# An adaLN block with a mixture of experts: a reordered last shared group, later down weights, tables in the experts' program, last tiles with kept numbers and in halves

## The reference

```python
h = _layernorm(x) * (1 + cb) + sb
scores = sigmoid(h @ gate_w + bias)
top_scores, top_idx = top_k(scores, 2)            # of 8 experts
top_scores = top_scores / (sum(top_scores) + 1e-06)
hact = gelu(h @ up_w[e] + up_b[e])                # per chosen expert, 256 -> 1024
eo = hact @ down_w[e] + down_b[e]                 # 1024 -> 256
shared = (gelu(h @ sw_up + sb_up) @ sw_down + sb_down) * 0.1
out = shared + sum(top_scores * eo * 0.1)
out = out / (max(abs(out)) + 1e-06)               # over the 256 numbers of a token
x = x + gb * out
```

## Time and profile before

| | us |
|---|---|
| median of 3 runs | 877.2 (875.07 to 881.87) |
| the profiled execution | 877.31 |
| its span | 875.4 |
| TensorE busy in the span | 828.9 (95%) |
| VectorE, ScalarE, POOL busy | 611.5, 455.1, 458.6 |
| mean granted TensorE clock | 0.978 of full speed |

### The profile page before, as it was taken

The page is one execution under the profiler, slowest core; times in us unless marked ns, Lnnn a source line. Parts: engine busy times, 40 slices in busy tenths (PEclk is TensorE's granted clock), DMA queues, the critical chain, the costliest instruction groups (busy, mean ns, idle before and its releaser), DMA issues.

```text
span 875.4 us, 21221 instructions
## 1 busy us (share of the span) xinstructions
PE 828.9 (95%) x5973; PEld 776.9 (89%) x5974; DVE 611.5 (70%) x1566; ACT 455.1 (52%) x859; POOL 458.6 (52%) x521
## 2 busy tenths in 40 slices
PE   6999999899999999999799999989999999999982
PEld 5778887889889989987799999979999999999982
DVE  5788988668777777767847566666666666666653
ACT  3865654244443544445476555565566555556630
POOL 4554320224765765675204656646656665665565
PEclk9999999899999999999999999989999999999996
DMA  8220000381242243232652333434433343444442
GB/s 300 75 97 1 1 0 1 89 253 25 101 125 38 88 123 77 67 103 91 227 198 76 89 88 98 147 96 94 94 86 86 87 93 93 92 92 86 86 89 52
DMA packets 68491, 83.25 MB, mean 95 GB/s; under 512 B 22976, under 2 KB 56730, under 8 KB 68288
## 3 DMA queue, kind: packets, MB, share of 16 engines
q0 software_dynamic: 25792, 39.92, 19.6%
q1 hardware_dynamic: 41808, 41.64, 15.1%
q10 hardware_dynamic: 816, 0.79, 0.3%
HBM read 45.43 MB, written 41.55 MB: 99 GB/s over the span
## 4 chain that ended last, share of the span: by engine, by line
PE 28%; issue 7%; DVE 4%; DMA 3%; ACT 3%; POOL 2%; DVEq 2%; ACTq 1%; POOLq 0%
PE psUp L1971 14%; PE psY L1996 13%; DMA gx<-shared_part,meta 2%; ACT gu L2034 1%; DVEq L995 1%; DMA shared_part<-ys,widx 1%; POOL out L2243 1%; PE psH L1943 1%; DVE gTl L2099 1%; ACT gTh L2039 1%; DVE yc L2120 1%; DVE top L2138 1%; POOL shared_part L2233 1%; DVE fin L2147 0%; ACTq L995 0%
## 5 line engine op out<-in xcount | busy, mean ns | idle before, releaser
L1971 PE MATMUL psUp<-eT,wup 128*128 128x256 f32 x1632 | 206.3, 287 | 5.5 <-DVE eT L2094 4.2
L1971 PEld LDWEIGHTS psUp<-eT,wup 128*128 128x128 f32 x1632 | 202.2, 195 | 6.5 <-issue 6.3
L1996 PE MATMUL psY<-wdn,gTh 128*128 128x256 f32 x1088 | 200.5, 286 | 0.0
L1996 PEld LDWEIGHTS psY<-wdn,gTh 128*128 128x128 f32 x1088 | 169.4, 192 | 0.0
L1996 PE MATMUL psY<-wdn,gTl 128*128 128x256 f32 x544 | 154.3, 284 | 0.0
L2243 POOL DMA_INDIRECT out<-fin,oidx x68 | 109.3, 1608 | 23.2 <-issue 15.9
L2034 ACT ACTIVATE gu<-psUp,ubias 128x256 f32<-128x256 f32 x272 | 113.4, 468 | 8.0 <-DVE gTl L2099 4.1
L2053 ACT ACTIVATE ys<-yc,meta 128x256 f32<-128x256 f32 x68 | 31.0, 503 | 162.6 <-DVE yc L2120 162.6
L2233 POOL DMA_INDIRECT shared_part<-ys,widx x68 | 71.4, 1050 | 79.5 <-issue 49.6
L2099 DVE TENSOR_TENSOR gTl<-gu,gTh 128x512 fp32r<-128x512 f32 x136 | 93.7, 689 | 27.4 <-ACT gTh L2039 24.7
L2224 POOL DMA_INDIRECT gx<-shared_part,meta x68 | 68.0, 1001 | 84.0 <-DMA shared_part<-ys,widx 62.3
(11 more groups left out here) (325 smaller groups left out, 1392.2 us busy)
## 6 DMA issues: line engine op xcount, KB each, us to landing
hin<-expert_in SPq DMA_DIRECT2D x36, 256.0 KB
X<-in_L_attn_x SPq DMA_DIRECT2D x8, 512.0 KB, 7.8
X<-bo_row POOLq DMA_DIRECT2D x8, 512.0 KB, 5.6
shared_part<-prow SPq DMA_DIRECT2D x8, 512.0 KB, 6.0
shared_part<-sh SPq DMA_DIRECT2D x8, 512.0 KB
out<-X SPq DMA_DIRECT2D x8, 512.0 KB, 4.3
raw_up<-in_L_ffn_up_w SPq DMA_DIRECT2D x3, 1024.0 KB, 5.6
raw_dn<-in_L_ffn_down_w SPq DMA_DIRECT2D x3, 1024.0 KB, 9.7
```

Of the source, the lines that this page charges most:

```text
L1971: mm = nc.tensor.matmul(psU[:, c, (m % 2) * TR:(m % 2 + 1) * TR], wup[s][:, a, k, m * P:(m + 1) * P], eT[:, u, b, k], start=(n == 0), stop ...
L1996: mm = nc.tensor.matmul(psE[:, u, h * C:(h + 1) * C], (gTh, gTl)[a][:, u, m, h * P:(h + 1) * P], wdn[s][:, b, m], start=(n == 0), stop=(n ...
```

## The change

It has these parts.

1. In the last shared group TensorE takes `up(3)` ahead of `rank()`. ScalarE takes the sigmoid after `gelu(1)`, not after `gelu(0)`, and the splits of the first expert's `raw_up` after `gelu(6)` and `gelu(7)`. VectorE's order changes as the diff shows, and `pos_ok` is given by `choose_rest`.
2. SP asks for `raw_dn` of the first expert behind the two loads of rows. In the experts' program it loads the rows of tile 2 and the last 16 numbers of each row of tile 1 (`meta`) first, then the second expert's weights, then the biases; the biases are waited for by tile 0's result.
3. `table_used`, `table_slots` and `table_next` run in the experts' program, after `low(0, 0)`. The engines wait for `tab_ok` 4 there, and tile 0 takes slot 0 without reading a table. `iota_h` is made in the shared program.
4. From tile 32 on, `known` keeps an entry in a register, so that it is read once on an engine; TensorE and VectorE read some of them ahead.
5. The last tile's end works by halves of 128 rows (`finish`): `g_in` is a semaphore per half, and POOL issues the first half's `out` when `fin` of that half is ready. POOL writes a tile's `ys` only if another tile follows, and ScalarE leaves the last tile's out.

```diff
-    def weights(sp, e):
+    def weights_up(sp, e):
         sp.dma_start(raw_up[:], up_v[bass.ds(e, 1)].rearrange("a p k n -> p (a k) n")).then_inc(up_in, 16)
+
+    def weights_dn(sp, e):
         sp.dma_start(raw_dn[:], down_v[bass.ds(e, 1)].rearrange("a p k n -> p (a k) n")).then_inc(dn_in, 16)
...
                 else:
                     up(2)
+                    up(3)
                     rank()
-                    up(3)
                     down(0)
                     down(1)
                 if ffn_on:
...
                     for m in range(MK):
                         gelu(m)
-                        if m == 0:
+                        if m == 1:
                             act.wait_ge(mx_ok, f + 1)
                             nc.scalar.activation(sg[:], mx[:, :, 0:TOPK].rearrange("p t k -> p k t"), ACT.Sigmoid
                                                  ).then_inc(sg_ok, 1)
-                        if m in (5, 6):
-                            split_hi(act, 0, 0, (0,), (m - 5,))
+                        if m >= MK - 2:
+                            split_hi(act, 0, 0, (0,), (m - MK + 2,))
                     return
...
-                    nc.vector.tensor_tensor(h2[:, r, :, C + 1:C + 1 + E], wd[:, 0], wd[:, 1], ALU.add)
+                    step(nc.vector.tensor_tensor(h2[:, r, :, C + 1:C + 1 + E], wd[:, 0], wd[:, 1], ALU.add))
+                    settled()
+                    assert n[0] == ROUTE + 5
+                    nc.vector.sem_inc(pos_ok, 1)
...
                 if not att_on:
                     gate_copy()
+                    shared_read(f - 1)
                     gate_read()
                     tops()
                     places()
                     choose_two()
-                    choose_rest()
-                    place()
-                    shared_read(f - 1)
                     low_g(0)
                     low_g(1)
+                    place()
+                    choose_rest()
                     low_g(2)
-                    dve.wait_ge(rt_dve, ROUTE * NG + 4)
                     table_experts()
                     low_g(3)
                     table_spans()
                     low_g(4)
                     table_rows()
                     low_g(5)
-                    table_used()
+                    low_g(6)
                     split_lo(dve, 0, 0, (0,), (0,))
-                    low_g(6)
-                    table_slots()
                     low_g(7)
-                    table_next()
                     split_lo(dve, 0, 0, (0,), (1,))
                     return
                 second = isinstance(g, int) and g == 1
...
-            weights(sp, entry(sp, etab, 0, E - 1))
+            e_first = entry(sp, etab, 0, E - 1)
+            weights_up(sp, e_first)
...
             for j in range(2):
                 load_rows(sp, first_rows[j], j)
+            weights_dn(sp, e_first)
...
+    def known(eng, table, j, most):
+
+        if not isinstance(j, int) or j < FULL:
+            return entry(eng, table, j, most)
+        key = (eng.engine, table.name, j)
+        for old in [k for k in held if k[0] == eng.engine and k[2] < j - 2]:
+            del held[old]
+        if key not in held:
+            held[key] = entry(eng, table, j, most)
+        return held[key]
...
             load_tails(sp, entry(sp, rtab, 0, E * REG - TR), 0)
             sp.wait_ge(sh_ev, 2 * NG)
             sp.dma_start(shd_v[:, TG * (NG - 1):NT, :], sh[:]).then_inc(sh_st, 16)
+            rows(2, 0)
+            tails(1, 1)
+            sp.wait_ge(tab_ok, 3)
+            e = entry(sp, ntab, 0, E - 1)
+            with sp.If_ne(sp.to_reg(e), 0):
+                sp.wait_ge(w_ok, 1)
+                weights_up(sp, e)
+                sp.wait_ge(w_ok, 2)
+                weights_dn(sp, e)
+            sp.wait_ge(tab_ok, 4)
             sp.dma_start(dbias[:], down_b.partition_broadcast(P)).then_inc(db_in, 16)
-            ahead(0)
             tiles(sp, body)
...
-                k_exp = entry(pe, ktab, j, E)
+                if isinstance(j, int) and j == 0:
+                    return 0, 0
+                k_exp = known(pe, ktab, j, E)
                 if isinstance(j, int) and j >= FULL:
-                    return entry(pe, stab, j, 2), k_exp
+                    return known(pe, stab, j, 2), k_exp
...
+            pe.wait_ge(tab_ok, 4)
 
             def body(j, u, more, i):
+                soon = isinstance(j, int) and FULL - 2 <= j < ET - 2
+                if soon:
+                    known(pe, stab, j + 2, 2)
                 if more:
                     up(j + 1, 1 - u)
+                if soon:
+                    known(pe, ktab, j + 2, E)
                 down(j, u, more, i)
 
             tiles(pe, body)
...
                 wait(dve, ey_mm, j + 1)
+                if isinstance(j, int) and j == 0:
+                    dve.wait_ge(db_in, 16)
                 if later(j, 1):
...
+            def finish(j, u, landed, h, e):
+
+                done = 3 * j + 3 * h
+                wait(dve, g_in[u][h], landed)
+                if not h:
+                    wait(dve, s_ok, 2 * j)
+                    wait(dve, f_s, 2 * j)
+                nc.vector.tensor_tensor(bs[:, h], gx[:, u, h, C:2 * C], gx[:, u, h, 0:C], ALU.add).then_inc(b_ok, 1)
+                wait(dve, ey_ev, j + 1)
+                wait(dve, b_ok, j + 1 + h)
+                nc.vector.scalar_tensor_tensor(sm[:, h], yc[:, h], meta[:, u, h, bass.ds(e + 1, 1)], bs[:, h],
+                                               ALU.mult, ALU.add).then_inc(s_ok, 1)
+                wait(dve, s_ok, 2 * j + h + 1)
+                nc.vector.tensor_reduce(top[:, 0, h:h + 1], sm[:, h], AX.X, ALU.max, apply_absolute_value=True
+                                        ).then_inc(f_c, 1)
+                wait(dve, f_c, done + 1)
+                nc.vector.tensor_scalar(top[:, 0, h:h + 1], top[:, 0, h:h + 1], EPS, None, ALU.add).then_inc(f_c, 1)
+                wait(dve, f_c, done + 2)
+                nc.vector.reciprocal(top[:, 1, h:h + 1], top[:, 0, h:h + 1]).then_inc(f_c, 1)
+                wait(dve, f_c, done + 3)
+                nc.vector.scalar_tensor_tensor(fin[:, u, h], sm[:, h], top[:, 1, h:h + 1], gate_fb[:],
+                                               ALU.mult, ALU.mult).then_inc(f_s, 1)
 
             def last(j):
 
-                start(j, j % 2, j // 2)
-                end(j, j % 2, False)
+                u, i = j % 2, j // 2
+                e = known(dve, etab, j - 1, E - 1)
+                result(j - 1, 1 - u, e)
+                for h in range(2):
+                    finish(j - 1, 1 - u, 16 * i + 16 * u, h, e)
...
+                if isinstance(j, int) and j >= FULL:
+                    known(dve, etab, j, E - 1)
                 targets(j, u, i)
...
             low(0, 0)
-            split_lo(dve, 0, 0, (1,))
-            for c in range(MC):
-                if c == 2:
-                    low(1, 1)
-                low_g(0, 0, c)
-            dve.wait_ge(db_in, 16)
-            dve.wait_ge(io_ok, 1)
+            table_next()
+            table_slots()
+            low_g(0, 0, 0)
+            split_lo(dve, 0, 0, (1,), (0,))
+            low(1, 1)
+            low_g(0, 0, 1)
+            split_lo(dve, 0, 0, (1,), (1,))
+            low_g(0, 0, 2)
+            low_g(0, 0, 3)
+            dve.wait_ge(tab_ok, 4)
             tiles(dve, body, last)
 
...
             def body(j, u, more, i):
+                def parts():
+                    wait(pool, y_ok, 2 * j + 2)
+                    for h in range(2):
+                        wait(pool, g_in[u][h], 16 * i + 16)
+                    for h in range(2):
+                        first = bass.IndirectOffsetOnAxis(ap=widx[:, u, h:h + 1], axis=0)
+                        nc.gpsimd.indirect_dma_start(out=sx_half[:, :], out_offset=first, in_=ys[:, u, h], in_offset=None,
+                                                     bounds_check=2 * N - 1, oob_is_err=False).then_inc(w_st[u], 16)
+
                 wait(pool, ix_ok, 2 * j + 2)
-                wait(pool, y_ok, 2 * j + 2)
-                wait(pool, g_in[u], 32 * i + 32)
-                for h in range(2):
-                    first = bass.IndirectOffsetOnAxis(ap=widx[:, u, h:h + 1], axis=0)
-                    nc.gpsimd.indirect_dma_start(out=sx_half[:, :], out_offset=first, in_=ys[:, u, h], in_offset=None,
-                                                 bounds_check=2 * N - 1, oob_is_err=False).then_inc(w_st[u], 16)
                 if not isinstance(j, int) or j + 1 < FULL:
+                    parts()
                     gather(j + 1, 1 - u, i + u)
                 elif more:
                     with needed(pool, j + 1):
+                        parts()
                         gather(j + 1, 1 - u, i + u)
-                wait(pool, f_s, 2 * j + 2)
                 for h in range(2):
+                    wait(pool, f_s, 2 * j + 1 + h)
```

130 lines of the change are left out of this document (68 added, 62 removed).

## The result

The changed kernel took 869.09 us (median of 4 runs, 866.89 to 872.56) beside 877.55 us for the kernel before: a ratio of 0.9906, 95% interval 0.9877 to 0.9935, or 8.5 us less. A second set of 6 runs gave 868.26 us and a ratio of 0.9904 (0.9871 to 0.9936). The prediction was 867.6 us with a range of 864.0 to 872.5.

A forecast was written before the change was run, and what follows sets the result against it. TensorE, busy in most of the program, was taken as the bound, leaving only its idle or low-clock places and the closing gathers; 4.3 - 0.3 + 5.6 = 9.6 us off gave 867.6 us, range 864.0 to 872.5.

The forecast's parts named there:

- Part 1, the last shared group: Last shared group: reordering removes TensorE's waits for `gf` and `glo`, ending its shared work 3.3 to 3.5 us sooner.
- The price on POOL: Last shared group: `pos_ok` comes later, so POOL's last scatters start 1.5 us later.
- Part 2, the border: Border between the two programs: fewer VectorE tables and later `raw_dn` bring the first transposes 4.3 us sooner, bounds 3.0 and 5.3.
- The choice for the bandwidth of the strip and against packets in turn: Border: moving `raw_dn` frees bandwidth for the scatters; under packet turns the border would gain only about 3 us.
- Part 3, the first expert tiles: First expert tiles: moved tables and later `raw_dn` cost 0.3 us, bounds 0 and 2.5.
- rival (b): First expert tiles: `raw_dn` lands 2 us late or TensorE's clock falls after waiting; 2.5 us more, 870.1; chance 0.18.
- the tables are just hidden: First expert tiles: 5.6 us of VectorE tables fit behind up(0) at the lower clock, with up(1) at 10.5 to 10.9.
- Part 4, the end: End after tile 32: fewer register loads and the last tile by halves gain 5.6 us, bounds 3.5 and 7.
- Rival (c): End: a branch costs, not a load; POOL's longer jump takes 4.38 us, giving 870.4; chance 0.10.
- The gathers are: End: the last chain waits for tile 33's gathers, not TensorE's end; they land 1.6 us sooner, at 856.75 and 859.7.
- (a): Border: the rows stay late behind `raw_up` or a `pos_ok` costing 3 us; gain only 2, 869.9; chance 0.16.
- (d): First expert tiles: `raw_dn` lands 13.5 us after the transposes, making the kernel slower than before, above 877.2; chance 0.03.

The follow-up runs named there:

- one_piece: The changed kernel with the last tile's sum, scale and out in one piece over both halves again: 870.15 us, ratio 0.9924 to the kernel before.
- dn_early: The changed kernel with the first expert's `raw_dn` asked for directly behind `raw_up` again, ahead of the rows: 867.57 us, ratio 0.9882 to the kernel before.
- changed_again: The changed kernel itself run a second time, nothing altered: 868.26 us, ratio 0.9904 to the kernel before.
- the six: Six profiles of the changed kernel and variants with its whole new front; up(1) came 11.3 to 12.9 us behind the first transposes.
- gelu_first: The changed kernel with ScalarE's first Gelu chunks and `eT` ahead of the `raw_dn` splits, and VectorE's `low(1, 1)` directly behind the tables: 867.34 us, ratio 0.9865.

## Why the prediction was right, and where it was not

**The sum.** 4.3 - 0.3 + 5.6 = 9.6 us were predicted; the stretches of the changed kernel give 5.1 - 1.0 + 6.3 = 10.4 with the first tiles counted up to tile 4, and the runs 8.5. The time was right within 1.5 us, with some luck: 2 of the 6.3 us are POOL's last jump, which was in no term, and they make up for a gap that hardly closed and for first tiles that cost more than was said. Of the profile's 8.0 us, 5.1 lost at the start and 2.7 won by the clock in the loop are in no term either. The lower end of the range does not follow from the bounds: 5.3 and 7 us are 12.3, which gives 864.9 and not 864.

**Part 1, the last shared group: right.** No wait for `gf` or `glo` is left (one of 0.7 us for `glo` in `one_piece` and `dn_early`), and TensorE ended its shared work 23.4 us behind the gate instead of 27.3, 3.9 sooner where 3.3 to 3.5 were said. The price on POOL was half of what was said: the last group's scatters began 8.7 us behind the gate, 7.9 before, so 0.8 us later and not 1.5.

**Part 2, the border: right, 5.1 for 4.3.** The step that was too small is that of SP: `hin` was issued 21.1 us behind the gate, 1.1 us sooner than the 22.2 that the prediction's 426.9 amounts to, because the last scatter started 17.5 us behind the gate and not 18.7. The choice for the bandwidth of the strip and against packets in turn was right (`dn_early`: 1.9 us at the transposes), though nothing of the 1.9 was left at up(1). That two of the three edits can bring 0.8 or 0.5 us of the 5.1 was in the words "four engines must come to the barrier" but in no number. None of the three was run alone.

**Part 3, the first expert tiles: the right runner, mis-sized.** "Issued at about 428.0 behind 0.5 MB of rows it should land after 5 to 6 us, 3.9 us after the transposes" is the step that failed: `raw_dn` took 7.2 us and came 5.2 us behind them, and in `changed_again` 8.6 and 6.8. ScalarE waited 3.95 and 5.52 us for it, and past 4 us was named as a sign of being wrong. Set against 10.7 before, up(1) came 0.6 to 2.2 us later, 1.4 in the mean of the six, and in four of them the clock fell to 0.66 behind the wait, which is rival (b)'s second half. At tile 4 the six are 43.3 us behind their transposes in the mean, the three kernels with the old front 41.2: 2.0 us instead of 0.3, within the bound of 2.5. The sentence that each us of delay is lost was right in direction; a part came back as waits ahead of up(2) and up(3) that are not there in the late profiles. The claim that the tables are just hidden holds; `gelu_first` has them all and up(1) at 9.8.

**Part 4, the end: a near sum, from steps of which two were wrong.** "With numbers kept and loaded ahead ... the gap falls by some 2 us" failed: it fell by 0.4, since most of the gap was a jump and the loads ahead of it lay beside it. Only the one load behind the jump was saved, 0.8 us, and the jump ended 0.4 us later behind tile 32. Rival (c) had the mechanism, a branch that waits for instructions, but put it on POOL, whose jumps stayed short:

```profile
L1870 POOLq COMPARE_BRANCH  x6: 34/40/55, 832.5 to 866.7; - x6
```

"The gathers are" what the last chain waits for failed too: they landed early enough, and TensorE's `yc` at 856.23 gated the tail. `yc` of tile 32 came 2.3 us sooner, behind its matmuls, where 1.6 was said. One half's chain was 2.5 us from `bs` to the end of `fin`, as worked out. And 2 us came from POOL's last jump in the kernel before, which stood in no step: the 2.8 us between that jump and the end could have been asked about.

**The rivals.** (a) fell: the rows were early. (b) came true for the most part: 2.0 us at tile 4, of its 2.5 and the forecast's 0.3 together. (c) was the true mechanism at another place. (d) fell: `raw_dn` was at worst 6.8 us behind the transposes.

## What to carry to other kernels

Where several engines meet at a barrier, work out the arrival of each before and after: an edit that moves one is worth only the distance to the next, and here any two of three edits brought 0.5 to 3.2 us, all three 5.1. Then follow the gain for some tiles: the last 1.9 of the 5.1 were gone at the next wait. A wait of an in-order engine for a transfer should stand behind all the work that others need from that engine; with two Gelus and a low part ahead of the splits up(1) came 2.3 us sooner, of which 0.7 was left at tile 4. And an idle time put down to "issue" behind a branch is to be read in the sequencer's rows, branch by branch, before it is given to the loads that stand beside it.

## What the runs showed of the hardware that was not expected

- A jump held TensorE's queue for 2.60 us at one place and 0.06 to 0.35 us at 129 others of the same line. The same jump took 2.1 to 3.3 us in the seven other profiles with the same loads ahead. With two more loads ahead it took 0.8 to 1.2 us and ended no later (1.4 to 1.7 us behind tile 32, against 1.3 to 2.5). Behind POOL's last jump the span went on for 2.8 us in the kernel before and 0.7 us in the changed kernel and in `before_padded` (870.7 to 871.4), where 15 idle instructions stood ahead.
- A gap of TensorE cost more than itself. Behind gaps of 2.7 and 3.4 us the granted clock over the next 10 to 12 us was 0.84 and 0.72; without the gap it was 1.00 and down(33) ended 4.4 us sooner. Behind one of 2.5 us (`one_piece`) and one of 3.1 (`before_padded`) it was 1.00 as well, so the length of the gap alone does not decide it. Behind waits of 2.4 to 4.3 us ahead of up(1) it was 0.66 over the next 5 us in all four profiles, behind waits of 1.4 to 1.6 us 1.00 in all four.
- The slower of the last tile's two indirect gathers of 128 rows took 3.4 to 3.7 us in five profiles and 4.0 to 6.8 us in the nine others. With TensorE out of the way this decides the last 2 us, and no run here shows its cause.
